# Expert tiles taken in pairs, second-layer products as 64-row halves, combine weights matched on VectorE

## The chip, the cores and the metric

One core of one Trainium2 chip runs one program. The metric is device time in microseconds from start to end of an execution, as the median over runs. The five engines named below are TensorE (PE, with its weight loads PEld), VectorE (DVE), ScalarE (ACT), GpSimd (POOL) and SyncE (SP), whose queue issues most transfers.

## The reference

A pre-norm decoder layer on x of shape (16, 128, 256), float32: `x + attention(norm(x))`, then cross attention over a context, then a mixture of experts. Only the last concerns the change:

```python
probs = softmax(x @ gate_w)                      # 2048 tokens, 64 experts
topk_w, topk_idx = top_k(probs, 8); topk_w /= sum(topk_w)
for each expert: hdn = silu(x @ gw) * (x @ uw)   # 256 -> 64
                 acc += combine[:, e] * (hdn @ dw)   # 64 -> 256
out = acc + sigmoid(x @ shared_gate) * shared_expert(x)
```

## The kernel before

The experts are computed sparsely. For each batch r of 128 tokens the router finds the top 8 experts, and GpSimd scatters the 128 normalised rows eight times, by indirect DMA, into the experts' blocks of the table xs (`cross_pool`, line 1824; 128 scatters, of which at most two are under way). A scatter's slot is the expert's start plus the token's rank in it, and the slots of batch r come from VectorE (`route_slots`).

The rows are then taken in 192 tiles of 128 rows: tiles 0 to 63 are the first blocks of the 64 experts (the pair order runs from the last experts to the first), tiles 64 to 191 the further blocks, wherever they lie; three small tables (line 2031, kept in line 2037) hold for each of these the first row and the places of its weights, which SyncE and TensorE load into registers (lines 2197 and 2227). SyncE loads a pair of tiles (`load`, lines 2154 and 2157) into one of four buffers. TensorE turns a tile (`turn`, L2237, two transpositions), ScalarE copies it to x_turned, TensorE makes gate and up side by side (`up`, L2247), ScalarE applies silu, VectorE multiplies (L2325), TensorE turns the hidden values (`turn_hidden`, L2256), VectorE copies them (L2331), TensorE multiplies them by the second-layer weights (`down`, L2264), ScalarE copies the rows to y_tile (L2306), and SyncE stores a pair (`store`, L2162) to the table ys, six pairs behind its loads. A float32 product is two passes on TensorE, a transposition one.

down_res holds the second-layer weights of an even expert on partitions 0 to 63 and of the odd one on 64 to 127. The hidden product is written twice, so that its transposition fills 128 rows; line 2331 multiplies it by 1 or 0 per half (`par`), and a product of 128 rows with both experts' weights gives the one wanted.

The order is written out by hand in loops over j, the tile, one for each engine: in iteration j TensorE turns tile j, makes up(j - 1), turn_hidden(j - 3), down(j - 5). VectorE's loop also holds the sorting of the output rows (`combine_rows` at j = 20), eight reductions of weights found by GpSimd, every sixth iteration, the shared expert's gates and the combines.

Output rows go back by 128 gathers (`combine_pool`, L2403): gather g = 8r + k takes the k-th expert's rows of batch r from ys, with at most three under way. Batch r needs the stores of the first 36 + 4r pairs; a ring of 32 tiles receives them. VectorE adds them to X with their weights (`combine`, L2459). Before the gathers GpSimd turns slots into rows of ys (lines 2371 to 2381, from tables that SyncE loads at pairs 4 and 8; the load for pair 8 stands behind its wait for `row_steps`) and, for each k, finds the weights by comparing with the sorted rows (lines 2388 to 2390). SyncE loads down_res (`between_loads`, L2474) after the last cross-attention product.

## Time and profile before

| what | value |
|---|---|
| median of 3 runs (lowest to highest) | 999.36 us (995.24 to 1002.95) |
| profiled execution, first to last instruction | 1000.0 us (no other time of it is given) |
| mean granted clock of TensorE | 0.895 of 2.4 GHz |
| busy: PE, PEld | 810.3, 640.0 us |
| busy: DVE, ACT, POOL | 654.2, 533.3, 581.4 us |
| chain that ended last | DMA 26%, PE 19%, POOL 7% |
| largest piece of the chain | scatters to xs, 19% |

Busy time is summed over the whole span, whose stages have different limits: a scatter stage until 694 us, a tile stage, and gathers. A matmul's duration in the rows is longer than its share of the stream, since matmuls overlap; what counts is the distance from one start to the next. In a timeline a row merges neighbours of one kind: start, length from first start to last end, engine, line, operation, output and inputs, count, and in brackets the idle time before it and what ended it.

### The profile page before, as it was taken

To read this page: it belongs to the slowest core of one execution; us is meant where nothing else is said; L and a number is where in the kernel's file an instruction comes from. 1 tells how busy PE (TensorE), PEld (TensorE's weight loads), DVE (VectorE), ACT (ScalarE), POOL (GpSimd) and SP (SyncE) were. 2 spreads that over 40 slices of the span, in tenths; PEclk is the share of its full clock that TensorE was granted. 3 is DMA by queue.
4 is the path that set the end of the run, shared out by engine and by line. 5 is a ranking of instruction groups with operands and counts; after the bars stand their busy time and mean duration, and the time that the engine had idled before them with its cause. 6 is when DMAs were issued, how large, how long until landed. Compare 5 with 4: busy or idle time off the path is not lost.

```text
span 1000.0 us, 21154 instructions
## 1 busy us (share of the span) xinstructions
PE 810.3 (81%) x6280; PEld 640.0 (64%) x6311; DVE 654.2 (65%) x1963; ACT 533.3 (53%) x1373; POOL 581.4 (58%) x768
## 2 busy tenths in 40 slices
PE   5988999999999999877787865224899999989702
PEld 3766777777777777655555533113789988888601
DVE  6747778787887786987777743241456567666545
ACT  2424677667766776655554443112567777666400
POOL 3685657666767862005653445465699355555665
PEclk9987999999999999989888887555999999999955
DMA  6200212222222113645547654524767799989635
GB/s 153 61 21 17 70 49 83 66 69 83 71 66 71 45 43 78 144 102 159 165 151 229 212 169 148 192 85 155 236 207 217 220 295 297 280 273 283 200 99 158
DMA packets 128908, 143.03 MB, mean 143 GB/s; under 512 B 25619, under 2 KB 114262, under 8 KB 128798
## 3 DMA queue, kind: packets, MB, share of 16 engines
q1 hardware_dynamic: 116510, 108.11, 36.6%
q0 software_dynamic: 12288, 33.57, 10.7%
q8 instruction: 55, 0.90, 0.4%
q14 instruction: 55, 0.45, 0.2%
HBM read 78.54 MB, written 62.93 MB: 141 GB/s over the span
## 4 chain that ended last, share of the span: by engine, by line
DMA 26%; PE 19%; POOL 7%; issue 7%; DVE 4%; ACT 1%; SPq 0%; POOLq 0%; another core or an unknown queue 0%; DVEq 0%; ACTq 0%
DMA xs<-xrow,slot_idx 19%; PE bank L2247 6%; PE bank L2264 5%; DMA got_rows<-ys,slot_idx 5%; POOL got_rows L2403 4%; PE bank L2237 3%; DVE xmax L1514 2%; POOL xs L1824 1%; PE bank L2256 1%; PE bank L1504 1%; PE bank L1581 1%; DMA ctx_in<-xs 1%; PE bank L1606 1%; DMA got_rows<-row_tables 0%; DVE X L2459 0%
## 5 line engine op out<-in xcount | busy, mean ns | idle before, releaser
L1824 POOL DMA_INDIRECT xs<-xrow,slot_idx x128 | 123.5, 965 | 111.9 <-DMA xs<-xrow,slot_idx 101.5
L2403 POOL DMA_INDIRECT got_rows<-ys,slot_idx x128 | 123.3, 963 | 92.0 <-DMA got_rows<-ys,slot_idx 45.3
L947 ACT ACTIVATE probs<-bank 128x512 f32<-128x512 f32 x192 | 113.9, 604 | 85.2 <-PE bank L759 48.1
L2247 PE MATMUL bank<-up_res,x_turned 128*128 (+1 forms) x768 | 121.0, 281 | 5.5 <-DVE hid_s L2325 5.0
L2325 DVE TENSOR_TENSOR hid_s<-gate_s,bank 128x128 f32<-128x128 f32 x192 | 54.8, 286 | 106.8 <-ACT gate_s L2299 105.5
L2264 PE MATMUL bank<-down_res,hid_t 128*128 (+1 forms) x384 | 114.8, 381 | 0.1
L1681 ACT ACTIVATE probs<-bank 128x512 f32<-128x512 f32 x128 | 75.6, 612 | 68.0 <-PE bank L1581 67.6
L2247 PEld LDWEIGHTS bank<-up_res,x_turned 128*128 128x128 f32 x768 | 103.1, 195 | 7.8 <-issue 5.9
L1514 DVE TENSOR_REDUCE xmax<-bank 128x2 f32<-128x512 f32 x128 | 85.2, 687 | 34.4 <-PE bank L1504 34.4
L2293 ACT COPY x_turned<-bank 128x256 f32<-128x256 f32 x192 | 72.5, 377 | 37.7 <-PE bank L2237 37.5
L2459 DVE SCALAR_TENSOR_TENSOR X<-got_rows,left,X 128x256 f32<-128x256 f32 x128 | 61.7, 482 | 40.9 <-DMA got_rows<-ys,slot_idx 38.2
L757 PE MATMUL bank<-query,keys 128*128 128x256 f32 x256 | 82.7, 347 | 0.5 <-ACT probs L947 0.4
L1504 PE MATMUL bank<-keys_x,query_x 112*128 112x256 f32 x256 | 58.6, 316 | 29.9 <-DVE xmax L1514 29.9
L1070 DVE TENSOR_REDUCE blockmax<-bank 128x32 f32<-128x512 f32 x96 | 63.1, 686 | 26.7 <-PE bank L709 25.5
L1504 PEld LDWEIGHTS bank<-keys_x,query_x 112*128 112x128 f32 x256 | 50.8, 212 | 41.3 <-DVE xmax L1514 32.5
L1581 PE MATMUL bank<-query_x,keys_x 114*128 114x512 f32 x128 | 68.5, 535 | 4.4 <-ACT probs L1681 4.1
L2306 ACT COPY y_tile<-bank 128x256 f32<-128x256 f32 x128 | 47.7, 373 | 40.9 <-PE bank L2264 40.4
L2331 DVE TENSOR_SCALAR hid_t<-bank,par 128x128 f32<-128x128 f32 x192 | 66.1, 344 | 0.1
L2264 PEld LDWEIGHTS bank<-down_res,hid_t 128*128 128x128 f32 x384 | 58.0, 191 | 0.9 <-issue 0.7
L1221 POOL TENSOR_TENSOR key_a<-keyT,kv_rows 64x512 bf16<-64x512 f32 x16 | 16.6, 1037 | 69.5 <-ACT keyT L900 69.5
L757 PEld LDWEIGHTS bank<-query,keys 128*128 128x128 f32 x256 | 49.2, 192 | 7.9 <-ACT probs L947 0.9
L2256 PE MATMUL bank<-ident,hid_s 128*128 128x128 f32 x192 | 52.7, 274 | 0.0
(366 smaller groups left out, 2158.1 us busy)
## 6 DMA issues: line engine op xcount, KB each, us to landing
ys<-y_tile SPq DMA_DIRECT2D x64, 256.0 KB
xs<-zero_b SPq DMA_DIRECT2D x16, 512.0 KB, 3.2
ys<-xn SPq DMA_DIRECT2D x32, 256.0 KB
up_res<-in_w_up SPq DMA_DIRECT2D x6, 1280.0 KB, 7.4
keys_x<-key_rows_x SPq DMA_DIRECT2D x32, 192.0 KB
ctx_in<-in_ctx SPq DMA_DIRECT2D x32, 128.0 KB, 2.4
key_rows_x<-ctx_hi SPq DMA_DIRECT2D x256, 16.0 KB, 1.5
query_x<-xq_rows_hi SPq DMA_DIRECT2D x64, 64.0 KB
```

The lines of the kernel that those rows point to most:

```text
L757: nc.tensor.matmul(o, keys[p][:, kvh * 4 + j, :], query[p][:, kvh, 256:512], start=True, stop=False)
L947: nc.scalar.activation(probs[:, u, :], SCORE[u % 2][:], ACT.Exp, scale=SCALE)\
L1504: last = nc.tensor.matmul(max_bank(g)[:, n * D:n * D + D], query_x[s][0:XROWS, k, pair // 2, c * 128:c * 128 + 128], keys_x[s][0:XROWS, k, ...
L1514: nc.vector.tensor_reduce(xmax[b % 2][:, m // 4, hs:hs + 2], max_bank(XH * b + m)[:].rearrange("p (h n) -> p h n", h=2), AX, ALU.max).then ...
L1581: nc.tensor.matmul(XSCORE[n % 2][:].rearrange("p (t m) -> p t m", t=2), keys_x[s][0:XROWS + 2, k, c * 128:c * 128 + 128], query_x[s][0:XRO ...
L1681: nc.scalar.activation(probs4[b % 2][:, u, :], XSCORE[n % 2][:], ACT.Exp, scale=XSCALE)\
L1824: nc.gpsimd.indirect_dma_start(out=xs, out_offset=bass.IndirectOffsetOnAxis(ap=slot_idx[:, r, k:k + 1], axis=0), in_=xrow[r % XROW_RING][: ...
L2247: last = nc.tensor.matmul(bank[2 + j % 2][:, 0:128], x_turned[j % 2][:, c * 128:c * 128 + 128], w[:, 256 * c:256 * c + 192].rearrange("p ( ...
L2264: nc.tensor.matmul(bank[6 + j % 2][:, 0:D], hid_t[j % 3][:], down_weights(j), start=True, stop=True).then_inc(S("tile_down"), 1)
L2293: nc.scalar.copy(x_turned[j % 2][:], bank[j % 2][:, 0:D]).then_inc(S("tile_kept"), 1)
L2331: nc.vector.tensor_scalar(hid_t[j % 3][:], bank[4 + j % 2][:, 0:128], par[:, 0, j:j + 1], None, ALU.mult).then_inc(S("tile_hidT"), 1)
L2403: nc.gpsimd.indirect_dma_start(out=got_rows[:, g % GOT_RING, :], out_offset=None, in_=ys[0:T * (E + 8 * r + 8), :], in_offset=bass.Indirec ...
```

## The change

The tile loops run over 96 pairs instead of 192 tiles: one keep (512 columns), one silu, one hidden product and one hidden copy for a pair, two buffers of each. The hidden product is written once per tile. In a pair of first blocks one transposition turns both tiles' hidden values, the even one's to partitions 0 to 63, the odd one's to 64 to 127, and `down` issues two products of 64 rows, one on each half, into different banks. In the other pairs each tile's hidden values are turned separately to partitions 0 to 63, and both second-layer products use that half; for these the odd experts' weights are loaded a second time to the lower half. The even tile's rows are copied by ScalarE, the odd one's by VectorE. The `par` table and what makes it are gone.

The weights of the combine are found on VectorE in the order of the slots (`match_weights`): 32 chunks of four batches and one k, 24 before the tile loop and one in each of iterations 2 to 9. So that the later sort of the output rows keeps that order, a multiple of 32768 per expert is added to the row's number and masked off again (`row_places`). The ring of gathers has 16 places instead of 32, a gather of k = 0 or 4 waits for the combine 12 before, and each combine waits for its own gather.

```diff
-ROWS_AT, WEIGH_GAP, COMBINE_AT = 20, 6, 97
-HIDDEN_AT, ADD_AT = 76, 104
+NP = TILES // 2
+GOT_RING = 16
+CHUNK = 4
+EARLY_CHUNKS, CHUNKS = 24, 32
+CHUNKS_AT, ROWS_AT, HIDDEN_AT, COMBINE_AT, ADD_AT = 2, 15, 24, 46, 90
+ROW_KEY = 32768
+Y_BEHIND = 7
...
             def down_weights(j):
-                return down_res[:, ds(256 * first_pair(j // 2) if j < E else down_at[j - E], 256)]
+                if j < E:
+                    return down_by[I * (j % 2):I * (j % 2) + I, first_pair(j // 2), j % 2, :]
+                return down_res[0:I, ds(down_at[j - E], 256)]
...
+            def turn_hidden(p):
+                pe.wait_ge(S("tile_hidden"), ended("tile_hidden") + p + 1)
+                if p >= 2:
+                    pe.wait_ge(S("tile_hidT"), ended("tile_hidT") + p - 1)
+                if 2 * p < E:
+                    nc.tensor.transpose(HID_TURNED[p % 2][:, 0:T], hid_s[p % 2][:].rearrange("p a i -> p (a i)"),
+                                        ident[:]).then_inc(S("tile_hid_turned"), 1)
+                    return
+                for a in range(2):
+                    last = nc.tensor.transpose(HID_TURNED[p % 2][0:I, T * a:T * a + T], hid_s[p % 2][:, a, :],
+                                               ident[:])
+                last.then_inc(S("tile_hid_turned"), 1)
+
+            def down(p):
...
+                pe.wait_ge(S("tile_hidT"), ended("tile_hidT") + p + 1)
+                if p:
+                    pe.wait_ge(S("tile_y"), ended("tile_y") + p)
+                if p >= 2:
+                    pe.wait_ge(S("tile_y_odd"), ended("tile_y_odd") + p - 1)
+                for a in range(2):
+                    turned = hid_t[p % 2][I * a:I * a + I, 0, :] if 2 * p < E else hid_t[p % 2][0:I, a, :]
+                    nc.tensor.matmul((Y_EVEN, Y_ODD[p % 2])[a][:, 0:D], turned, down_weights(2 * p + a),
+                                     start=True, stop=True).then_inc(S("tile_down"), 1)
...
+            for i in range(NP + 3):
+                if i < NP:
+                    values(i)
+                    turn(i)
+                if 0 <= i - 1 < NP:
+                    up(i - 1)
+                if 0 <= i - 2 < NP:
+                    turn_hidden(i - 2)
+                if 0 <= i - 3:
+                    down(i - 3)
...
+            for n in range(EARLY_CHUNKS):
+                match_weights(dve, n)
             g = 0
+            for i in range(1, NP + 4):
+                if i - 1 < NP:
+                    hidden(i - 1)
+                if 0 <= i - 2 < NP:
+                    hidden_turned(i - 2)
+                if 0 <= i - 4:
+                    rows_odd(i - 4)
+                if 0 <= i - CHUNKS_AT < CHUNKS - EARLY_CHUNKS:
+                    match_weights(dve, EARLY_CHUNKS + i - CHUNKS_AT)
...
+                while g < 8 * NS and COMBINE_AT + 18 * g // 25 <= i:
                     combine(dve, g)
                     g += 1
...
-            for k in range(8):
-                out = (a, c)[k % 2]
...
-                link(nc.gpsimd.tensor_tensor(out, v, t, ALU.subtract))
-                link(nc.gpsimd.tensor_scalar(out, out, 0.0, None, ALU.is_equal))
-                nc.gpsimd.tensor_tensor(out, out, routed[:, 0:NS, 0:E], ALU.mult).then_inc(S("weight_found"), 1)
...
-                if k == 0 and g >= GOT_RING:
-                    pool.wait_ge(S("combined"), ended("combined") + g - GOT_RING + 8)
+                if k % 4 == 0 and g >= GOT_RING:
+                    pool.wait_ge(S("combined"), ended("combined") + g - GOT_RING + 4)
...
+        def match_weights(dve, n):
+            lo, k = CHUNK * (n // 8), n % 8
+            some = slice(lo, lo + CHUNK)
...
+            at = slot_top[:, some, k:k + 1].to_broadcast([128, CHUNK, E])
+            route_link(dve, nc.vector.tensor_tensor(found, slot_of[:, some, :], at, ALU.is_equal))
+            route_link(dve, nc.vector.tensor_tensor(found, found, routed[:, some, 0:E], ALU.mult))
+            nc.vector.tensor_reduce(weigh[:, some, k], found, AX, ALU.add).then_inc(S("weight_taken"), 1)
...
+            def load_down(k, a, side, name):
+                some = slice(4 * k, 4 * k + 4)
+                sp.dma_start(down_by[I * side:I * side + I, some, a, :], halves[:, some, a, :]).then_inc(S(name), 16)
+
             for k in range(8):
...
+                if k == 6:
+                    sp.wait_ge(S("xpv_done"), B)
+                for a in range(2):
+                    load_down(k, a, a, "ld_down_res")
+            for k in range(8):
+                load_down(k, 1, 0, "ld_down_swap")
```

## Rows read from the trace of the kernel before

**Rows 1.** Stretches: length, busy us (instructions) of PE, PEld, DVE, ACT, POOL; clock; DMA; GB/s

```profile
820.00:860.00 40.00, 39.89 (x296) 35.98 (x294) 28.20 (x92) 28.30 (x99) 21.86 (x23) 1.00 0.94 291
960.00:1000.00 40.00, 7.68 (x16) 4.65 (x16) 21.00 (x40) 0.00 (x0) 23.53 (x25) 0.50 0.46 137
```

**Rows 2.** Chain of waits: start us, us, what; then TensorE's timeline at pair 8

```profile
691.50 2.88 DMA xs<-xrow,slot_idx
694.86 4.52 DMA got_rows<-row_tables
704.83 2.37 POOL got_rows L2376
707.60 5.48 DMA ctx_in<-xs
...
713.12 0.44 PE L2237 MATMUL bank<-ident,ctx_in 128*128 128x128 f32 x2 [1.55 <-DMA ctx_in<-xs]
```

**Rows 3.** TensorE's timeline, one tile: start us, us, engine, line, operation, count

```profile
760.60 0.38 PE L2237 MATMUL bank<-ident,x_tile 128*128 128x128 f32 x2
760.82 0.61 PE L2247 MATMUL bank<-up_res,x_turned 128*128 128x128 f32 x4
761.26 0.27 PE L2256 MATMUL bank<-ident,hid_s 128*128 128x128 f32 x1
761.37 0.60 PE L2264 MATMUL bank<-down_res,hid_t 128*128 128x256 f32 x2
761.80 0.38 PE L2237 MATMUL bank<-ident,x_tile 128*128 128x128 f32 x2
```

**Rows 4.** Timelines of SyncE's queue and GpSimd: the store and the first gather

```profile
789.01 0.38 SPq L2162 DMA_DIRECT2D ys<-xn  x1
...
792.01 1.06 POOL L2403 DMA_INDIRECT got_rows<-ys,slot_idx  x1 [13.91 <-DMA ys<-xn]
```

**Rows 5.** Gathers, line 2403: stretches with POOL busy (count); the line's durations

```profile
790.00:938.20 148.20, 83.95 (x88) 1.00 0.90 277
938.20:993.40 55.20, 39.32 (x41) 0.57 0.48 143
...
L2403 POOL DMA_INDIRECT got_rows<-ys,slot_idx x128: 940/946/1205, 792.0 to 992.4; - x128
```

**Rows 6.** Line 509: durations min/median/max ns, first and last start us, form

```profile
L509 PE MATMUL bank<-kv_masked,w x128: 374/374/478, 53.3 to 60.2; 32*128 32x256 f32 x128
```

**Rows 7.** TensorE's timeline in the shared expert

```profile
941.57 0.63 PE L2105 MATMUL bank<-ident,routed 128*64 128x128 f32 x4
942.13 1.99 PE L2120 MATMUL bank<-down_sh,up_res 64*128 64x256 f32 x8
944.05 0.63 PE L2105 MATMUL bank<-ident,routed 128*64 128x128 f32 x4
```

**Rows 8.** TensorE's waits from 713 to 938: total us, times, longest

```profile
PE bank L2247 <- DVE hid_s L2325: 5.0, 5, 1.8
```

**Rows 9.** Scatters, line 1824, by stretch: POOL busy (count), clock, DMA, GB/s

```profile
620.40:635.50 15.10, 4.79 (x5) 0.66 0.99 329
635.50:648.00 12.50, 8.64 (x9) 0.50 0.24 85
```

**Rows 10.** VectorE: first hidden product in its timeline; line 2077's durations

```profile
690.66 0.29 DVE L2325 TENSOR_TENSOR hid_s<-gate_s,bank 128x128 f32<-128x128 f32 x1 [23.66 <-ACT gate_s L2299]
...
L2077 DVE TENSOR_TENSOR routed<-routed,sig x4: 424/425/426, 794.1 to 808.8; 128x256 f32<-128x256 f32 x4
```

**Rows 11.** VectorE's timeline; chain of waits with GpSimd's issues beside it

```profile
952.06 4.15 DVE L2459 SCALAR_TENSOR_TENSOR X<-got_rows,left,X 128x256 f32<-128x256 f32 x8 [5.68 <-DMA got_rows<-ys,slot_idx]
...
951.60 0.95 POOL got_rows L2403
952.85 1.03 POOL got_rows L2403
954.19 0.96 POOL got_rows L2403
```

More of the change, by code:

```diff
@@ L1385, in build @@
         tiles_3 = sb("tiles_3", [3, EXTRA], I32)
[L1386 to L1390 removed]
+        tables_at.close()
+        place[0] = place.pop()
+        got_rows = sb("got_rows", [128, GOT_RING, D])
+        x_last = sb("x_tile3", [128, 2, D])
+        x_turned1 = sb("x_turned1", [128, 2 * D])
+        gate_s = [sb(f"gate_s{n}", [128, 2, I]) for n in range(2)]
+        hid_s = [sb(f"hid_s{n}", [128, 2, I]) for n in range(2)]
+        hid_t = [sb(f"hid_t{n}", [128, 2, T]) for n in range(2)]
         place[0].close()
@@ L2181, in sparse_loads @@
             batch_sent(sp, NS - 2)
-            for p in range(TILES // 2):
+            for p in range(NP):
                 if p < 4:
@@ L2202, in sparse_loads @@
                 load(p)
-                if p >= 6:
-                    store(p - 6)
-            for p in range(TILES // 2 - 6, TILES // 2):
+                if p >= Y_BEHIND:
+                    store(p - Y_BEHIND)
+            for p in range(NP - Y_BEHIND, NP):
                 store(p)
@@ new lines, in up @@
+            def up(p):
+                pe.wait_ge(S("tile_kept"), ended("tile_kept") + p + 1)
+                if p >= 2:
+                    pe.wait_ge(S("tile_hidden"), ended("tile_hidden") + p - 1)
+                for a in range(2):
+                    w = up_weights(2 * p + a)
+                    for c in range(2):
+                        both = w[:, 256 * c:256 * c + 192].rearrange("p (t i) -> p t i", i=I)[:, 0:3:2, :]
+                        last = nc.tensor.matmul(bank[2 + p % 2][:, 2 * I * a:2 * I * a + 2 * I],
+                                                x_turned[p % 2][:, a * D + c * 128:a * D + c * 128 + 128], both,
+                                                start=c == 0, stop=c == 1)
+                last.then_inc(S("tile_up"), 1)
@@ L2301, in rows_out, with keep @@
-            def rows_out(j):
-                act.wait_ge(S("tile_down"), ended("tile_down") + j + 1)
-                n = len(y_tile)
-                if j % 2 == 0 and j // 2 >= n:
-                    act.wait_ge(S(f"y_out{j // 2 % n}"), 16 * (j // 2 // n))
-                nc.scalar.copy(y_slot(j), bank[6 + j % 2][:, 0:D]).then_inc(S("tile_y"), 1)
-            for j in range(TILES + 6):
-                if 0 <= j - 6 < TILES:
-                    rows_out(j - 6)
-                if j < TILES:
-                    keep(j)
-                if 0 <= j - 1 < TILES:
-                    gate(j - 1)
+            def keep(p):
+                act.wait_ge(S("tile_turned"), ended("tile_turned") + p + 1)
+                if p >= 2:
+                    act.wait_ge(S("tile_up"), ended("tile_up") + p - 1)
+                nc.scalar.copy(x_turned[p % 2], X_TURNED[:]).then_inc(S("tile_kept"), 1)
@@ L2315, in sparse_scalar @@
+            for i in range(NP + 4):
+                if 0 <= i - 4:
+                    rows_even(i - 4)
+                if i < NP:
+                    keep(i)
+                if 0 <= i - 1 < NP:
+                    gate(i - 1)
             for n in range(4):
@@ L2449, in combine @@
                 dve.wait_ge(S("weights_ready"), ended("weights_ready") + 1)
-            if k == 0 and r < NS - 1:
-                for last in range(8 - GOT_AHEAD, 8):
-                    got_until(dve, g + last)
-            if r == NS - 1:
-                got_until(dve, g)
+            got_until(dve, g)
             if g:
```

311 lines of the change are left out of this document (138 added, 173 removed).

## The prediction

> **What bounds the kernel now.** I read the stretches of the span first [rows 1] (the loop holds the full clock and fills the DMA engines; behind it TensorE is nearly idle), then the chain of waits that ended last [rows 2], then single engines. Up to about 694 us the chain is GpSimd's 128 row scatters, each waiting for an earlier one; then three table loads and GpSimd's row arithmetic, which holds back the load of pair 8 (issued at 707.60, landed at 713) [rows 2]. From 713.1 to 938.2 TensorE runs the expert tiles almost without a gap at the full clock: from tile to tile 1.20 to 1.21 us, made of two transpositions (0.22), four first-layer passes (0.44), one hidden transposition (0.11) and two second-layer passes (0.43) [rows 3]. A pair of tiles is thus 2.42 us. The gathers of output rows start at 792.01, 3.0 us after the store of pair 35 was issued (at 789.01) [rows 4]; 88 of them are issued until 938.2 while the DMA engines are 90% busy, and 40 remain, at 1.36 us each (the last issue at 992.4) [rows 5]. So two things set the end: when the first 36 pairs are stored, and when the last pair is done. Everything else has slack.
>
> The span of 1000.0 us is 0.6 us above the median of the three runs; I make the sum against the span and take 0.6 off.
>
> **1. Second layer of the first 32 pairs, side by side.** Removed: one hidden transposition per pair, 0.11 us. Two products of 128 rows (4 passes of 0.2155, 0.86 us) become two of 64 rows on different halves of the array. Does the array run them together? The nearest row is the compression layer: 128 passes of 32-row products in four row groups, 256 columns each, start between 53.3 and 60.2 us [rows 6], one every 0.054 us, a quarter of 0.2155. I take two passes in the time of one: -0.43 us per pair. Bounds: nothing (-0) and -0.43.
> The pages give another answer. The Trainium skill ("TensorE: Matmul & The Clock Gate", Part 3, "The mechanism") says that matmuls are strict first-in first-out and only weight loads are pulled ahead. By it the first pass of the odd tile starts only with the second pass of the even one, three slots instead of two, and a pair saves 0.22 instead of 0.43. The row above speaks against it, since every product there is two passes too.
>
> **2. What the 64-row form costs in a stream of 128-row work.** The trace of before has this neighbourhood once, in the shared expert: four transpositions, then eight 64-row passes, then transpositions again [rows 7]. From 941.57 to 944.05 are 2.48 us, where 4 x 0.109 + 8 x 0.2155 make 2.16. Going into 64-row form and out again costs 0.32 us that the streams of [rows 3] don't have. (The Trainium skill, "TensorEngine Tiling (Array Packing)", "Key Properties", says that changing the tiling mode drains the engine; the rows give the price.) The new order does this once in every iteration, because the second layer of one pair stands between the hidden transposition of another and the turning of a third. Bounds: 0 to 0.35 (the weights behind it are 128 columns wide here, 64 there). I take 0.32.
> It is paid in all 96 pairs: the 64 extra tiles' pairs too use 64-row second-layer products, but both on the lower half, so nothing runs side by side. For them one hidden transposition of 128 columns becomes two of 64 (0.109 each in [rows 7]), two per pair as before.
> So a pair of first blocks takes 2.42 - 0.11 - 0.43 + 0.32 = 2.20 us, an extra pair 2.42 + 0.32 = 2.74 us.
>
> **3. The loop.** Pair 8 can't start earlier than today: its load stands on SyncE's queue behind the wait for GpSimd's row steps, and these hang on the scatters and the table loads, not on TensorE [rows 2]. What is gained in pairs 0 to 7 is therefore lost in that wait. From iteration 8: 27 iterations gain 0.22 (-5.9 us), and 64 (35 to 98) lose 0.32 (+20.5). TensorE waited 5.0 us for VectorE in five places [rows 8], mostly where VectorE stood in a combine that wants three gathers of a batch at once; the new combine follows 9 or more gathers behind its own, so I take 4.5 of it away. Sum **+10.1 us** on the last pair. The store of pair 35 (iterations 8 to 38) comes 5.9 - 1.3 = 4.6 earlier.
>
> **4. Second weight copy.** The second-layer weights now come in 24 loads of 256 KB instead of 8 of 512 KB: 2.1 MB more. While the 4.2 MB of before moved (620.4 to 635.5), GpSimd issued 5 scatters; in the 12.5 us after them 9 [rows 9]. Each loaded scatter takes 3.0 us, an unloaded one 1.4; half again as much data is 7.5 us more under load, 2.5 scatters slower by 1.6. But part of the loads now starts before the last cross-attention product, where other loads already slowed the scatters: I take **+2.8 us** (0 to 5). The scatters are the chain there, so all that follows moves.
>
> **5. Weights matched on VectorE.** Removed from GpSimd: 24 operations over the whole weight table, after which it waited 13.9 us for rows [rows 4], so it gains nothing at the end. Added to VectorE: 32 chunks of two products of 128x256 and one reduction. A product of this size is 0.425 us [rows 10]; for the reduction over as many elements I take the same, with the waits between them 1.36 us a chunk. 24 chunks, 33 us, stand ahead of the first tile, where VectorE idles from 667.0 to 690.7 [rows 10]. It comes 6 us late after the shift of part 4; then each of iterations 2 to 9 has 2.5 us of work on VectorE against 2.2 on TensorE. TensorE has room: pair 8 waits for its load anyway. Both come out within a microsecond of each other, so 0, with 3 us if the cover is short (queued behind the chunks are the hidden products, and TensorE's transpositions behind these).
> The chunks also meet the scatters. GpSimd's issue pitch goes from 1.25 to 1.34 us when VectorE combines two operands beside it [rows 11]; over the some 20 scatters of that time (28 us at 1.4) about **+1.0 us** (0 to 2). The Trainium skill ("GPSIMD Engine Reference", Specifications) names this contention for instructions of two SBUF inputs; it gives no price.
> The row key, the sorting in four parts, the smaller tables: a few operations of 0.2 us each beside TensorE's stream, 0. The copy of every odd tile's rows moves from ScalarE to VectorE; both are busy 28 of 40 us in the loop at its fullest [rows 1], and pairs halve the number of the other operations, so 0. One x_turned bank: its copy ends well before the next turning, 0. SyncE's store lies one pair further back but behind the same iteration, 0.
>
> **6. The tail.** The ring of 16 ties gather g to combine g - 12, and combines run at 18/25 iteration each, the last in the loop g = 74. So 88 gathers are out when the loop ends, as today, and 40 remain. The new waits are for single gathers, not batches: 1.30 instead of 1.36 us each, -2.4 us; and the last 9 combines, which today run back to back after 992.0, follow each landing, -1.4. **-3.8 us.**
>
> **Sum:** 1000.0 + 10.1 + 2.8 + 1.0 - 3.8 = 1010.1, less 0.6: 1009.5, written **1010 us**, about 1% slower.
>
> **Rivals.**
> (a) *The mode change is hidden* behind waits or weight loads in this stream. Then first pairs take 1.88, extra ones 2.42: -14.6 - 4.5 + 3.8 - 3.8 = -19.1 for the first sum; some 4 gathers more remain at the end (+5.2), since the loop is shorter than the gathers need: 1000 - 19.1 + 5.2 - 0.6 = 985.5, the other side. For it: each waiting product is issued long before it runs. Against it: [rows 7], at full clock and with their inputs ready. It decides below 0.10 us per iteration, where the loop's cost falls under its gain.
> (b) *Half the price*: 0.16 us per iteration, 995 us, no change.
> (c) *Strict order of passes*: 27 x 0.22 = 5.8 us more, 1015.
> (d) *VectorE becomes the bound* in iterations 2 to 10 or where chunks, sorts and combines meet: up to 6 us more, 1016; its busy time per pair leaves it little room early and a microsecond later.
> (e) *The change doesn't do what it says*: if the 64-row products don't run together at all, 27 x 0.43 more, 1021.
>
> **Chances.** My sum 0.47, (a) 0.18, (b) 0.17, (c) 0.08, (d) 0.06, (e) 0.04. The range 985 to 1020 takes in (a)'s centre, the bounds of parts 4 and 5 and (c), (d); my own case's range is 1002 to 1018. One per cent, about what a measurement of this kernel can tell from none, is 989.4 to 1009.4. My case lies on the upper edge: 0.30 of its 0.47 above, 0.17 within, where (b) lies too. Faster 0.18, within 1% 0.34, slower 0.48.
>
> **What would show it.** The start-to-start time of pairs: 2.20 for first blocks and 2.74 for extra ones (1.88 and 2.42 would be (a), 2.42 for the first (c)). Pair 8 near 717. The first gather near 791. The scatters' end at 698. VectorE's last early chunk near 700. The last tile near 952 with 88 gathers out. If the extra pairs take 2.42 us, I am wrong by the mode change; if pair 8 comes before 713, by the chain ahead of it.

## The result, and the profile after

The changed kernel takes **1028.33 us** (median of 4 runs, 1026.5 to 1033.1), the kernel before in the same job 1000.7 us: a ratio of **1.029, interval 1.025 to 1.034**. The prediction said 1010 and a range up to 1020: the direction was right, the size and the range were not. The two profiled spans are 1024.7 and 1000.0 us, so 24.7 us are to be placed. Four instants cut the span:

| | before | after | difference added by the stretch |
|---|---|---|---|
| last scatter issued | 691.5 | 703.1 | +11.6 |
| pair 8 turned | 713.1 | 725.5 | +0.8 |
| pair 9 turned | 715.6 | 730.1 | +2.0 |
| last expert product ends | 938.6 | 961.2 | +8.2 |
| end of the span | 1000.0 | 1024.7 | +2.1 |

**The scatters.** Two views of line 1834 (line 1824 before): the same two stretches, in the changed kernel and then before. Columns: POOL busy (number issued), clock, DMA share, GB/s.

```profile
609.00:643.00 34.00, 9.25 (x10) 0.59 1.08 236
643.00:690.00 47.00, 30.01 (x32) 0.50 0.26 90
```

```profile
609.00:643.00 34.00, 16.74 (x18) 0.64 0.64 209
643.00:690.00 47.00, 29.54 (x32) 0.50 0.27 93
```

Ten scatters in place of 18; behind them the rate is the same. Read share and rate together: the busiest part of before moved 329 GB/s at a share of 0.99 [rows 9], the changed kernel 236 GB/s at 1.08. The engines are fuller and move less. (With the loads of the changed kernel the last scatter came at 703.1, 700.6 and 699.2 us in three traces, in the kernel before at 691.5 and 690.1; so one trace places this term to within some 4 us.)

**The start of the loop.** VectorE's timeline of the changed kernel, and GpSimd's beside it:

```profile
677.94 0.40 DVE L2468 TENSOR_TENSOR got_rows<-slot_of,slot_top 128x256 f32<-128x256 f32 x1
...
711.00 0.47 DVE L2345 TENSOR_TENSOR hid_s<-gate_s,bank 128x128 f32<-128x128 f32 x2
...
717.61 1.25 DVE L2468 TENSOR_TENSOR got_rows<-slot_of,slot_top 128x256 f32<-128x256 f32 x1
718.89 2.46 DVE L2469 TENSOR_TENSOR got_rows<-got_rows,routed 128x256 f32<-128x256 f32 x1
721.39 0.42 DVE L2470 TENSOR_REDUCE count<-got_rows 128x4 f32<-128x256 f32 x1
721.73 0.28 DVE L2345 TENSOR_TENSOR hid_s<-gate_s,bank 128x128 f32<-128x128 f32 x1
```

```profile
716.23 2.35 POOL L2413 TENSOR_TENSOR got_rows<-got_rows 128x1024 f32<-128x1024 f32 x1
718.66 2.42 POOL L2415 TENSOR_TENSOR got_rows<-got_rows,slot_of 128x1024 f32<-128x1024 f32 x1
```

The 24 early chunks run until 711.0, though pair 0 was turned at 699.55 (690.66 was the first hidden product before [rows 10]). Then the chunks inside the loop meet GpSimd's row steps: the product of line 2469 takes 2.46 us in place of 0.42 and ends at 721.35, 0.27 us behind the end of GpSimd's operation (718.66 to 721.08). The product of line 2468 before it ends at 718.86, 0.28 us behind GpSimd's of 716.23 to 718.58. A hidden product is queued behind each. GpSimd's own operation is no longer than its neighbours.

Pair 8 hardly feels it. Its load is issued 15.9 us behind the last scatter (718.99; 16.1 in the kernel before), and it is turned 22.4 us behind the last scatter where it was 21.6. The next two chunk products, of 1.40 and 2.23 us, then hold up pair 9. The x buffers are used in the order ctx_in, ctx_hi, ctx_lo, x_tile, so ctx_in holds pair 8 and ctx_hi pair 9. TensorE in the changed kernel, and pair 9 in the kernel before:

```profile
725.54 0.66 PE L2240 MATMUL bank<-ident,ctx_in 128*128 128x128 f32 x4
...
728.80 0.33 PE L2262 MATMUL bank<-ident,hid_s 128*128 128x128 f32 x1 [1.71 <-DVE hid_s L2345]
729.42 0.70 PE L2282 MATMUL bank<-down_res,hid_t 64*128 64x256 f32 x4 [0.29 <-DVE xrow L2365]
730.06 0.66 PE L2240 MATMUL bank<-ident,ctx_hi 128*128 128x128 f32 x4
```

```profile
715.63 0.38 PE L2237 MATMUL bank<-ident,ctx_hi 128*128 128x128 f32 x2
```

The chain of waits runs there over VectorE (start, length, what) and releases pair 9, from which on every pair follows at its own pitch:

```profile
724.51 1.33 DVE got_rows L2468
725.87 2.25 DVE got_rows L2469
...
729.42 0.70 PE bank L2282 x4
```

**Pairs.** TensorE's timeline of the changed kernel, a first pair and an extra pair, to be read against [rows 3]:

```profile
762.56 0.27 PE L2262 MATMUL bank<-ident,hid_s 128*128 128x128 f32 x1
762.76 0.70 PE L2282 MATMUL bank<-down_res,hid_t 64*128 64x256 f32 x4
763.39 0.66 PE L2240 MATMUL bank<-ident,ctx_in 128*128 128x128 f32 x4
```

```profile
852.71 0.38 PE L2266 MATMUL bank<-ident,hid_s 128*64 128x128 f32 x2
853.02 1.13 PE L2282 MATMUL bank<-down_res,hid_t 64*128 x4
854.08 0.66 PE L2240 MATMUL bank<-ident,x_tile 128*128 128x128 f32 x4
854.57 1.06 PE L2252 MATMUL bank<-up_res,xrow 128*128 x8
```

Four passes side by side last 0.63 us from first start to the next operation, in series 1.06 us. So the halves of the array do work together. A 64-row pass itself is no slower than one of 128 rows: the eight passes of [rows 7] last 1.92 us and the four here 1.06, so four more cost 0.86, or 0.215 each. What the form costs lies at the change into it and out of it. Steady pairs follow each other every 2.222 us (first blocks) and 2.755 us (extra).

**The gathers**, line 2430 by stretch, up to the last product and behind it, and what GpSimd waited for at them (us, times); before are [rows 5]:

```profile
804.00:961.20 157.20, 84.01 (x85) 1.00 0.84 254
961.20:1019.00 57.80, 40.41 (x44) 0.58 0.47 142
```

```profile
L2430 POOL DMA_INDIRECT got_rows<-ys,slot_idx x128: 940/946/1201, 804.9 to 1018.9; - x128
...
  DVE X L2488: 31.3, 14
```

One gather (940/946/1201 ns) costs what it did, but from first to last issue they take 214.0 us, where they took 200.4. (A gather under way at 961.2 is counted in both stretches.) 31.3 us are waits for combines to give a buffer free; before these were 2.2 us. So a second way to add up the loss: first gather +12.9, the stream of gathers +13.6, behind it -1.8.

The first gather also stands further behind the loop than it did: 8.7 us behind the turn of pair 38, where it was 4.8 ([rows 4]; pair 38 turned at 787.21). It waits for the store of pair 35, and that store for VectorE's copy of the odd tile's rows, which the new loop makes one iteration behind ScalarE's copy of the even tile's (798.64). TensorE, VectorE and SyncE's queue in the changed kernel:

```profile
796.21 0.66 PE L2240 MATMUL bank<-ident,ctx_lo 128*128 128x128 f32 x4
...
801.40 0.40 DVE L2365 COPY xnT<-bank 128x256 f32<-128x256 f32 x1
...
801.88 0.38 SPq L2158 DMA_DIRECT2D ys<-xnT  x1
```

No run moved this copy, so what it costs in time is not shown.

### The profile page after: what moved, and what is told of

Read it like the earlier page. It is cut to its first block, busy times and chain, and to the rows that moved or that the text cites. A ratio compares the mean times of both kernels' runs of the same rounds, so it can differ in the third digit from the quotient of the medians.

```text
span 1024.7 us, 20489 instructions
## 1 busy us (share of the span) xinstructions
PE 820.2 (80%) x6246; PEld 619.4 (60%) x6277; DVE 675.3 (66%) x1947; ACT 483.4 (47%) x1085; POOL 529.1 (52%) x743
## 3 DMA queue, kind: packets, MB, share of 16 engines
q1 hardware_dynamic: 118814, 110.20, 37.1%
## 4 chain that ended last, share of the span: by engine, by line
PE 28%; DMA 17%; DVE 9%; issue 5%; POOL 4%; ACT 1%; POOLq 0%; another core or an unknown queue 0%; DVEq 0%; ACTq 0%
DMA xs<-xrow,slot_idx 16%; PE bank L2282 8%; PE bank L2252 8%; PE bank L2240 5%; POOL got_rows L2430 3%; DVE xmax L1524 2%; DVE got_rows L2469 2%; PE bank L2266 1%; DMA got_rows<-ys,slot_idx 1%; DVE got_rows L2468 1%; DVE count L2470 1%; POOL xs L1834 1%; PE bank L1514 1%; PE bank L1591 1%; PE bank L1616 1%
## 5 line engine op out<-in xcount | busy, mean ns | idle before, releaser
L2345 DVE TENSOR_TENSOR hid_s<-gate_s,bank 128x128 f32<-128x128 f32 x96 | 27.5, 287 | 105.6 <-ACT gate_s L2318 105.5
L2282 PE MATMUL bank<-down_res,hid_t 64*128 (+1 forms) x384 | 94.7, 411 | 0.8 <-DVE xn L2365 0.3
L2488 DVE SCALAR_TENSOR_TENSOR X<-got_rows,count,X 128x256 f32<-128x256 f32 x128 | 61.3, 479 | 30.6 <-DMA got_rows<-ys,slot_idx 26.1
L2282 PEld LDWEIGHTS bank<-down_res,hid_t 64*128 64x128 f32 x384 | 52.5, 185 | 22.7 <-issue 18.1
L2311 ACT COPY xrow<-bank 128x512 f32<-128x512 f32 x48 | 28.1, 585 | 56.4 <-PE bank L2240 56.4
L2252 PE MATMUL bank<-up_res,xrow 128*128 (+1 forms) x384 | 52.4, 281 | 0.0
L2252 PE MATMUL bank<-up_res,x_turned 128*128 (+1 forms) x384 | 51.2, 277 | 0.0
L2252 PEld LDWEIGHTS bank<-up_res,xrow 128*128 128x128 f32 x384 | 48.4, 198 | 0.0
L1875 PE MATMUL bank<-ident,xrow 128*128 128x128 f32 x32 | 9.9, 409 | 47.0 <-ACT xrow L1860 44.8
L2252 PEld LDWEIGHTS bank<-up_res,x_turned 128*128 128x128 f32 x384 | 47.1, 193 | 0.3 <-issue 0.3
```

Source lines behind the costliest of these rows:

```text
L2252: last = nc.tensor.matmul(bank[2 + p % 2][:, 2 * I * a:2 * I * a + 2 * I], x_turned[p % 2][:, a * D + c * 128:a * D + c * 128 + 128], both ...
L2282: nc.tensor.matmul((Y_EVEN, Y_ODD[p % 2])[a][:, 0:D], turned, down_weights(2 * p + a), start=True, stop=True).then_inc(S("tile_down"), 1)
L2488: nc.vector.scalar_tensor_tensor(X[:, r, :], got_rows[:, g % GOT_RING, :], weigh[:, r, k:k + 1], X[:, r, :], ALU.mult, ALU.add).then_inc(S ...
```

## The experiments

Theory: each loss above has its own cause (loads, chunks, 64-row products, the written-down pace of the combines). Rivals stand in the expectations. The code cuts are shortened. One slip runs through the expectations: the instants that they call pair 8's turn in a changed kernel (730.1, 724.0, 715.5) are those of pair 9, and only the 713.1 of the kernel before is pair 8's. Like goes with like at 715.6. The differences between changed kernels are not touched by it.

**Loads.** Run one: second copy later.

```
- for k in range(8): load_down(k, 1, 0, "ld_down_swap")      # between_loads
+ if p >= 10 and (p - 10) % 2 == 0 and (p - 10) // 2 < 8: load_swap((p - 10) // 2)   # sparse_loads, behind load(p)
```

> The eight loads of the second copy of the odd halves (2.1 MB to partitions 0 to 63) are moved from the stage of the scatters into the loop of pairs, one behind the x loads of pairs 10, 12, ... 24; the sixteen first-copy loads keep their form, 64 partitions each. The last scatter is issued at 691.5 us in the kernel before and 703.1 in the changed one. Theory A, the amount of data alone (6.3 MB in place of 4.2) held the scatters up: last scatter at 691 to 693, pair 8's turn at 718 to 720, the time some 11 us under the changed kernel's, about 1017. Theory B, the form of the loads (each to 64 partitions, so half as many partitions take twice the bytes) counts too: 4.2 MB at the 225 GB/s of the changed kernel last some 19 us, the scatters end at 695 to 699 and the time is about 1021 to 1024. Rival C, the scatters were held up by VectorE's early chunks and not by loads: no change, 703 and 1028. In the loop the eight moved loads should cost nothing, since the steady pair of 2.22 us is PE's own.

Measured: 1018.63 us, ratio 1.020 [1.017, 1.023]; last scatter 693.6, pair 9 at 720.7.

Run two: first copy to all partitions.

```
- for a in range(2): load_down(k, a, a, "ld_down_res")
+ sp.dma_start(down_by[:, some, 0, :], io["w_down"][some].rearrange("q p d -> p q d"))
  down_weights: down_by[I * (j % 2):..., first_pair(j // 2), 0, :]
```

> The sixteen first-copy loads of 256 KB to 64 partitions each become eight of 512 KB to all 128 partitions (the odd expert's rows of a pair now stand beside the even one's, in the same columns; the first pairs' second products read them there). The second copy stays where it is, eight loads to partitions 0 to 63. So the bytes are the same 6.3 MB, and 4.2 MB of them go in the form of the kernel before. Theory A (amount alone): last scatter still at 703, time about 1028. Theory B (form as well): the first 4.2 MB move at the 280 GB/s and more of the kernel before, the last 2.1 MB at about 225, the scatters end at 695 to 698, time about 1021. Rival C: no change.

Measured: 1023.02 us, 1.023 [1.021, 1.025]; last scatter 697.4, pair 9 at 724.6.

Run three: both edits.

> Both edits together: eight loads of 512 KB to 128 partitions in the stage of the scatters, as in the kernel before, and the second copy in the loop. Theories A and B both: the scatters end at 691.5 as before, the whole 11.6 us come back, the turn of pair 8 is at 718.5 (730.1 less 11.6) and the time about 1016 to 1017. Rival C (VectorE's early chunks held the scatters up): the last scatter stays near 703, the time near 1028. What is left over the kernel before, some 16 us, would then be the start of the loop (5), the extra pairs (6) and the tail.

Measured: 1014.08 us, 1.015 [1.012, 1.017]; last scatter 690.0, pair 9 at 715.5 (715.6 in the kernel before). The three kernels' scatters, in this order, in the stretch where the changed kernel issued 10:

```profile
609.00:643.00 34.00, 13.85 (x15) 0.61 0.79 197
```

```profile
609.00:643.00 34.00, 11.50 (x12) 0.64 0.87 248
```

```profile
609.00:643.00 34.00, 16.36 (x17) 0.60 0.58 201
```

Rival C falls: VectorE's early chunks stood in all of them. The whole delay is the loads' and comes back with them. From the corners of the four medians, the amount is worth 8.9 to 9.7 us of time and the form 4.6 to 5.3; run one lies nearer to the amount theory, the other theory's 695 to 699 was too late. The form also shows inside one trace. In run two the first copy goes to 128 partitions and then the second to 64, and here is a stretch of each (all five engines, then clock, DMA share, GB/s):

```profile
614.00:620.00 6.00, 1.71 (x14) 0.89 (x18) 0.00 (x0) 0.97 (x2) 1.92 (x2) 0.50 1.09 365
630.00:636.00 6.00, 0.00 (x0) 0.00 (x0) 0.00 (x0) 0.00 (x0) 0.96 (x1) 0.50 1.13 215
```

Smaller packets are not the reason: over the whole span the queue of the loads moves the same 110.20 MB in 118814 packets in run one and 118686 in run three. Why the same bytes take the engines longer when 64 partitions are written stays open.

**Chunks.**

```
- EARLY_CHUNKS, CHUNKS = 24, 32;  CHUNKS_AT, ROWS_AT, HIDDEN_AT = 2, 15, 24   # one chunk a step
+ EARLY_CHUNKS, CHUNKS = 18, 32;  CHUNKS_AT, CHUNK_STEP, ROWS_AT, HIDDEN_AT = 12, 2, 15, 25
```

> The loads stay as in the changed kernel. 18 early chunks stand ahead of the loop in place of 24, and the other 14 are matched at every second step from 12 on, behind GpSimd's six row steps; sorting, row places and the shared gates move to the odd steps behind them. Theory: the first hidden product no longer waits for 24 chunks until 711.0 (18 of 1.37 us end near 702.6), and no chunk meets a row step, which stretched the two-input operations from about 0.5 to 2.2 to 2.5 us. Pair 8 then turns 4 to 6 us earlier, at 724 to 726, and the time is 1022 to 1024. Rival, the chunks are covered and the start of the loop is set by the x loads behind the scatters: pair 8 stays at 730 and the time at 1028. Second rival, the 14 chunks in the loop make VectorE the bound of their pairs (1.37 plus about 1.1 us in a pair of 2.22): each costs up to 0.25 us, 3.5 us in all, and the time is 1026.

Measured: 1024.75 us, 1.025 [1.023, 1.028]; last scatter 700.6, pair 9 at 724.0, the first hidden product at 703.24 right behind its gate. The chunk's second product in the changed kernel and here (ns min/median/max):

```profile
L2469 DVE TENSOR_TENSOR got_rows<-got_rows,routed x32: 424/425/2465, 678.4 to 733.6; 128x256 f32<-128x256 f32 x32
```

```profile
L2471 DVE TENSOR_TENSOR got_rows<-got_rows,routed x32: 424/425/491, 674.7 to 793.4; 128x256 f32<-128x256 f32 x32
```

Away from GpSimd's row steps no product is longer than 0.49 us. From last scatter to pair 9 are 23.4 us in place of 27.0 (24.1 before). The 14 chunks in the loop cost no pair anything.

Loads and chunks together:

> The loads of both edits (first copy to 128 partitions, second copy in the loop) and the chunks moved (18 early, 14 at every second step from 12 on). With the loads mended the last scatter was issued at 690.0 us and pair 8 turned at 715.5; with the chunks moved pair 8 turned 23.4 us behind the last scatter (724.0 and 700.6) where it was 25.5 with the loads alone. Theory: the two are independent, pair 8 turns at 713.4, as in the kernel before (713.1), and the time is 1010.5 to 1012. What is left over the kernel before, some 11 us, is then all from behind pair 8: 64 pairs of 2.755 us and the tail. Rival, the x loads of the first pairs share the queues with something that the chunks had covered: pair 8 at 715 and no gain, 1014.

Measured: 1010.09 us, 1.012 [1.009, 1.015]; last scatter 687.7, pair 9 at 711.2: the start is that of the kernel before, or better (4.4 us earlier, of which 3.8 are an earlier last scatter). About 18 of the 28 us are explained by these two; the remaining 10 are from behind pair 9 (10.6 in the trace).

**Extra pairs without the change of mode.** The upper halves hold zeros and any weights:

```
- turned = hid_t[p % 2][0:I, a, :]                     down_res[0:I, ds(down_at[j - E], 256)]
+ turned = hid_t[p % 2][:, a, :]                       down_res[:, ds(down_at[j - E], 256)]
+ if 2 * p < E + 4: route_link(dve, nc.vector.memset(hid_t[p % 2][I:128], 0.0))   # first two extra pairs
+ load_swap: both halves, 16 loads
```

> The kernel with loads and chunks mended, and the second layer of the 64 extra pairs as products over all 128 rows: the upper 64 rows of the turned hidden tiles hold zeros, the second copy is loaded to both halves (16 loads in the loop), and PE no longer changes between 128-row and 64-row products in the extra pairs; the first pairs keep their two products side by side. Theory: of the 2.755 us of an extra pair, 0.32 to 0.34 are the way into the 64-row products and out of them; a pair is then 2.42 (two tiles of 1.209 in the kernel before), 64 x 0.335 = 21.4 us less, the last product ends at 923 to 925 and the time is about 989. Rival 1, the price is not of the change of mode but of a weight load that nothing hides, which 128 rows have as well: 2.6 us and more, 1000 or above. Rival 2, VectorE with its combines becomes the bound of the shorter pair: between 990 and 1000, with waits for hidden tiles in the trace.

Measured: 998.87 us, 1.000 [0.998, 1.003]. An extra pair in steady stream:

```profile
867.49 0.38 PE L2275 MATMUL bank<-ident,hid_s 128*64 128x128 f32 x2
867.71 1.03 PE L2291 MATMUL bank<-down_res,hid_t 128*128 x4
868.58 0.60 PE L2249 MATMUL bank<-ident,ctx_lo 128*128 128x128 f32 x4
869.01 1.06 PE L2261 MATMUL bank<-up_res,x_turned 128*128 x8
869.91 0.38 PE L2275 MATMUL bank<-ident,hid_s 128*64 128x128 f32 x2
```

The distance is 2.42 us (2.414 over many pairs), 0.34 under the changed kernel's. Into the products 0.22 us in place of 0.31, the products 0.87 in place of 1.06, the transpositions behind them 0.43 in place of 0.49: 0.34 in all. This settles the price: 64 x 0.34 = 21.8 us of TensorE's time. Rival 1 is dead. But only 11 of the expected 21 us arrived. Two reasons show. Pairs 9 to 24 lasted 2.5 to 3.3 us at eight places, 5.4 us too long in all, where the second copy (now 4.2 MB) passes; and the end is not the loop's any more. From first to last issue the gathers take 201.9 us, 12.5 less than with loads and chunks mended (214.4), and no less than before.

**The pace of the combines**, on the padded kernel and on the changed one:

```
- while g < 8 * NS and COMBINE_AT + 18 * g // 25 <= i:      COMBINE_AT = 46, ADD_AT = 90
+ while g < 8 * NS and COMBINE_AT + 1 * g // 2 <= i:        COMBINE_AT = 47, ADD_AT = 108
```

> The kernel with padded extra pairs, and the combines (and with them the 16 buffers that the gathers fill) at a quicker pace: combine g stands at step 47 + g/2 in place of 46 + 18g/25, so 104 of 128 are in the loop in place of 73. In the changed kernel 85 gathers were out when the last product ended, and the other 43 took 1.32 us each behind the loop. Theory: gathers, which went at 1.84 us each in the loop because they waited for buffers that VectorE had not combined yet, go at 1.25 to 1.45; some 104 to 110 are out at the last product's end, the tail is 20 x 1.32 = 26 us shorter, and the time is 960 to 968. Rival 1, the gathers are themselves the limit in the loop (a pair of 2.42 us asks for two combines, 1.21 us each, and 1.25 is the best pitch seen): VectorE waits for them and stalls PE, the loop lasts up to 10 us longer, and the time is 970 to 978. Rival 2, descriptors' making on GpSimd is slowed by VectorE's two-input combines: the pitch stays at 1.6 and more, and the time near 985.

> The changed kernel as it is, with the quicker pace of combines alone (47 + g/2; the shared products' adds from combine 108 on in place of 90). A pair of 2.755 us asks for a gather every 1.38 us, above the best pitch seen of 1.25. Theory: the 43 gathers behind the loop become some 22, 21 x 1.32 = 28 us less, and the time is 1000 to 1004, level with the kernel before. So the tail of the changed kernel, which should have become shorter, stayed because of the pace in which the combines are written down. Rival, the pace in the loop is that of the gathers (GpSimd's descriptors beside VectorE's two-input operations, 1.6 to 1.8 us each): VectorE then waits in the loop, PE stalls, and the time is 1020 or more.

Measured: 1002.49 us (1.003 [1.000, 1.005]) and 1012.43 us (1.015 [1.011, 1.019]). In both, 104 gathers are out when the last product ends, as expected, but that end is late: 964.8 and 971.8. The gathers by stretch, changed kernel with the quicker pace:

```profile
802.00:971.80 169.80, 101.55 (x104) 0.99 0.84 251
971.80:1003.00 31.20, 22.05 (x24) 0.50 0.59 176
```

And what VectorE waited for in the padded kernel with the quicker pace (us in total, times, longest):

```profile
DVE X L2501 <- DMA got_rows<-ys,slot_idx: 54.5, 49, 3.5
```

Rival 1 of both holds: VectorE stands in combines whose rows have not landed, and TensorE behind it. The stream of gathers lasts 200.4 and 200.5 us. In seven undisturbed traces (two of the kernel before, five with other paces or shorter pairs) it lasts 199.1 to 201.9 us, and in the six that keep the written pace at 2.755 us a pair 214.0 to 214.9. No pace brought it lower, so it acts as a floor: first gather, some 200 us of gathers, some 6 to 8 behind. The quicker pace alone gives back 16 us of the changed kernel's loss: 13.5 by the stream, the rest by a first gather that came 2.4 us earlier behind an earlier last scatter (699.2), which the pace has no hand in.

**Spread loads, a middling pace, four gathers under way.** Edits on the padded kernel: one load of the second copy behind each of the pairs 9 to 24; combine g at 46 + 2g/3; GOT_AHEAD 4 in place of 3.

> The kernel with padded extra pairs (998.9 us), where the sixteen loads of the second copy stand one behind the x load of each of the pairs 9 to 24 in place of two behind every second from 10 on. In the run before, pairs 9 to 24 lasted 2.5 to 3.3 us at 9 of 16 places, 5.4 us above 16 x 2.22 in all, and PE's waits there had no late engine beside them. Theory: SyncE's two loads in a row kept the store behind them back, and the buffers of y came free late; spread, the pairs last 2.22 to 2.4, the last product ends 3 to 5 us earlier against the last scatter, and the time is 994 to 996. Rival: the bytes themselves (4.2 MB beside x loads and stores) delay the stores wherever they stand: no change, 999.

> As the spread kernel, and combine g at step 46 + 2g/3 in place of 46 + 18g/25: 1.61 us to a gather at pairs of 2.414, beside the 1.63 that gathers reached in the loop when the combines asked for one every 1.21 us. Theory: gathers keep up just so, 86 to 88 are out at the loop's end in place of 82, each is worth the 1.35 us of one behind the loop, and the time is 4 to 7 us under the spread kernel's. Rival: every late gather now stops VectorE and with it PE, the loop grows by as much as the tail shrinks, and the time is the same within 2 us.

> As the kernel before it in this list, and GpSimd may have four gathers under way in place of three (the gather g waits for gather g-4). In the loop 28 to 39 us of its waits were for the third gather back. Theory: the landing of a gather is what sets the pitch, so with four under way it falls from 1.63 to 1.4 in the loop and from 1.37 to 1.25 behind it; the tail is 3 to 6 us shorter and the time 4 to 8 us less. Rival: the queues' work sets the pitch and not the latency, so that gathers land as late as before and wait longer: no change within 2 us.

Measured 1039.82, 1039.71 and 1045.51 us, beside a kernel before of 1081.35 (1078.8 to 1089.7): ratios 0.958, 0.961, 0.967. The kernel before is slow here too, so the cause is in none of the edits, and nothing of this job can be set beside 998.9. Within it the middling pace changes nothing and four gathers under way are 6 us slower. Two of the kernels once more, with the padded and the changed one:

> The spread kernel once more, on whichever chip comes. On the chip of the run before, the kernel before took 1081 us in place of 1000, so nothing of that run can be set beside the padded kernel's 998.9. Theory of the spread loads: 994 to 996 beside a kernel before of 1000, and 3 to 5 us under the padded kernel in this job. Rival: the same as the padded kernel within 2 us.

> The padded kernel once more, beside the spread one on the same chip. Expected 999 and a ratio of 1.00 to the kernel before where that takes 1000. Where the kernel before takes 1081, as on the other chip, 1040 to 1044 and a ratio of 0.96.

> The kernel with spread loads and combines at 46 + 2g/3 once more. Theory: 3 to 7 us under the spread kernel of this job, so 989 to 993 beside a kernel before of 1000. Rival: the loop grows by what the tail loses, the same as the spread kernel within 2 us, as on the other chip (1039.7 and 1039.8).

> The changed kernel itself in the same job, so that all five stand side by side. Where the kernel before takes 1000, a ratio of 1.029 as recorded. Where it takes 1081: the other chip's extra time lies, by the traces there, in the loop once gathers, stores and x loads run together, where PE waited for stores; a pair of 2.755 us leaves more room for transfers than one of 2.42, so the ratio should be smaller than 1.029, between 0.98 and 1.02.

Measured: 1038.84, 1030.12, 1028.46 and 1047.87 us, the kernel before 1073.68 (1056.9 to 1082.7), on a chip on which it had taken 999.4 in an earlier job. The changed kernel's ratio is 0.982 [0.966, 0.998] here: under 1, but by less than 2%, so unclear as a verdict. The spread loads are 9 us slower than the padded kernel in this job. In the trace of the changed kernel the early stages are 5.8 us late (pair 9 at 735.8, and still 5.8 at pair 42); some 20 us more lie in the loop from pair 42 on, when gathers run. The stretch 830 to 900 in the changed kernel, undisturbed and here (columns as in [rows 1]):

```profile
830.00:900.00 70.00, 70.00 (x461) 55.15 (x460) 38.47 (x110) 31.66 (x77) 37.31 (x37) 1.00 0.88 265
```

```profile
830.00:900.00 70.00, 62.70 (x380) 48.58 (x378) 32.67 (x93) 24.63 (x63) 31.06 (x32) 0.93 0.73 219
```

Fewer bytes at a lower share, and TensorE is idle for 7.3 of 70 us. A byte costs the DMA engines the same share in both (301 and 300 GB/s at a full share), so they are less used, not less efficient; what they wait for is not shown. A last job:

> Spread loads, padded extra pairs and combines at 46 + 2g/3. Where the kernel before takes 1000 us: 989 to 995, a ratio of 0.990 to 0.995, if the theories of the spread loads and of the pace both hold; 999 (1.00) if neither. Where it takes 1075: 1028 to 1040 again, a ratio of 0.96 to 0.97.

> The kernel before, traced in the same job. Where it takes 1000 the trace is the one shown ahead. Where it takes 1075, the trace tells where the 75 us lie: in the loop behind the first gather, as in the changed kernel (there +20 us of +25), if transfers are what is slow; in all stages alike, if it is a clock.

> Spread loads and padded extra pairs, the combines' pace as it was. Where the kernel before takes 1000: 994 to 996 if two loads in a row held the stores back, 999 if the bytes do. Where it takes 1075: 1039 again.

It was undisturbed: 1002.12 (1.002 [0.999, 1.006]), 999.96 (0.999 [0.996, 1.003]) and 1006.11 us (1.005 [1.001, 1.008]). The theory of two loads in a row asked for 994 to 996 and falls. What is left is its rival, the bytes, which no run varied by themselves in this kernel. DMA shares from pair 9 on, with 2.1 MB, 4.2 MB, and 4.2 MB spread:

```profile
711.00:762.00 51.00, 51.00 (x395) 39.62 (x391) 34.86 (x124) 27.75 (x69) 1.88 (x1) 1.00 0.93 279
```

```profile
709.00:760.00 51.00, 46.24 (x352) 35.85 (x351) 30.03 (x110) 23.70 (x62) 1.74 (x1) 1.00 1.03 297
```

```profile
719.00:770.00 51.00, 45.96 (x345) 35.00 (x342) 29.60 (x109) 21.71 (x61) 0.42 (x1) 1.00 1.05 287
```

At 0.93 TensorE has no gap, at 1.03 it loses 4.8 of 51 us. The middling pace gave 4 us against the spread kernel, and stays 3 us above the padded one's: no win. Four gathers under way was only tried in a disturbed job (stream 236.4 us against 232.4) and stays open, as does what holds the gathers at 200 us. No version beat the kernel before in an undisturbed job; the padded one equals it. Why the kernel before loses more than the changed one where transfers are slow stays open too: it was not caught in a trace there.

## Why the prediction was wrong

The forecast was +10.1 us on the span, the trace shows +24.7. The miss lies in two terms, step 4 (the second copy) and step 6 (the tail).

**Steps 1 and 2: right, to 0.02 us.** 2.20 and 2.74 us were forecast, 2.222 and 2.755 measured. Side by side holds, (a), (b) and (e) fall by it, and so does (c): the strict order of "TensorE: Matmul & The Clock Gate" in the Trainium skill would have shown first pairs of 2.42 us; the four passes in 0.63 us speak against it for products on different halves. The 0.32 us read from one place in the shared expert [rows 7] was the price of every iteration, as "TensorEngine Tiling (Array Packing)" in the Trainium skill lets expect of a drain; the padded pairs measured it again, 0.34.

**Step 3, the loop: +10.1 forecast, +10.2 measured, in part by luck.** From pair 8's turn to the last product are 225.4 us before and 235.6 after. Between the turns of pairs 9 and 95 and behind them 26 steps at 2.222 us gain 4.9, 60 at 2.755 lose 20.3 (0.338 each), and the last products run 1.6 us longer. The kernel before lost 8.8 us there to steps longer than its pitch of 2.417 us; the new loop loses nothing. I took away 4.5, from the one row of 5.0 us [rows 8]; the view of named waits under-counts such time, length less pitch times count gives it all. Against these 4.3 us too much stand 2.0 between pairs 8 and 9 that I did not foresee, and 2.4 by which pitches and last products come to more than my 14.6. The errors cancel.

**Step 4, the second copy: the failed step.** +2.8 us (0 to 5) forecast, +11.6 measured (8 to 12 with the other traces of these loads); with both edits of the loads 14.3 us of time come back, and the last scatter is where it was. I priced more data of the old form, and let some of it start early beside other loads for nothing. But each load now writes 64 partitions, and share and rate show that it moves fewer bytes in a full DMA time (236 GB/s at 1.08 against 329 at 0.99; inside one kernel 215 at 1.13 against 365 at 1.09). The early part was no relief either: the slow stretch runs from 609 to 643 us in place of 620 to 635. The upper bound of 5 was extrapolated from data alone; the form had no row before, and should have widened the range. The amount was under-priced too: the runs give it about 9 us and the form about 5.

**Step 5, the chunks: right up to pair 8, with 2 us behind it.** Cover 0 and contention 1.0 were forecast, +0.8 measured up to pair 8: its load is issued as far behind the scatters as before, and TensorE's stream, late by the chunks, comes to it within about a microsecond of its old place, as I had argued. The early chunks' duration was right (33 us from 677.9 to 711.0), their start was late by nearly the whole delay of the scatters. The contention I looked for stood at the wrong neighbour: not GpSimd's scatters, whose rate from 643 to 690 us is unchanged (32 in 47 us in both), but its row steps of 2.4 us, which stretch VectorE's two-input products to 2.46 us and make pair 9 2.0 us later. The Trainium skill's "GPSIMD Engine Reference" (Specifications) names this contention; the trace shows that in this meeting it was VectorE that paid. This is rival (d) in small, at its "2 to 10" iterations; moving the chunks gives 3.6 us back.

**Step 6, the tail: the second failed step.** -3.8 us forecast, +2.1 measured. I counted 88 gathers out and found 85, so the last gather is issued 57.7 us behind the last product in place of 53.9 (+3.8, where I had -2.4); behind it are -1.8, near my -1.4. The ring of 16 and the pace of 18/25 steps were in the text, but not that a step is 2.74 us in an extra pair: 0.72 x 2.755 = 1.98 us per combine, slower than the 1.67 at which the gathers went before. The ring turned the loop's slower steps into 31.3 us of waits, and the quicker pace takes them away (stream 200.5 us, span 1008.7). Of my rivals only (a) spoke of what the gathers themselves need, and only for a shorter loop.

Sum of the terms, in the prediction's order: +10.2 (loop) +11.6 (copy) +0.8 (chunks) +2.1 (tail) = 24.7, against +10.1 +2.8 +1.0 -3.8 = +10.1. The first two steps, on which I had put the doubt, were right; the terms about what lies around the loop made the miss.

## What to carry to other kernels

Price a load by its form as well as its bytes: DMA share and GB/s, read side by side, tell whether full engines also move much. When the rate of a loop changes, recompute every schedule that is written in its steps (here combines and, by a ring, gathers). After each repair ask which stream has the next longest run of its own: 21.8 us taken from TensorE brought 11, in part because in no run did the gathers take less than 199 us from the first on. And when two profiles are compared, check that an instant is the same pair in both, here by the name of its buffer.

## What the runs showed of the hardware

- A switch into 64-row products and back costs 0.34 us in a steady stream, where both sides are 128-row work: 0.09 on the way in, 0.19 from the first pass to the transpositions behind, 0.06 in these. Within the form further passes cost 0.215 us each, as at 128 rows. The same products padded to 128 rows cost nothing extra (2.414 us a pair, 2.417 before).
- Two-pass products on the two row halves, issued one after the other, ran together: four passes in 0.63 us against 1.06.
- Beside GpSimd operations over 128x1024 elements (2.4 us), VectorE's products of two SBUF inputs took up to 2.46 us in place of 0.42, ending 0.27 to 0.29 us behind GpSimd's end; GpSimd's six row steps took 14.6 us in all beside them and 14.4 in the kernel before.
- Loads that write 64 partitions moved 215 GB/s at a DMA share of 1.13, loads that write all 128 moved 365 at 1.09, in one kernel (run two); runs that differ in this form alone (one and three) moved the same bytes in as many packets to 0.1%.
- For whole jobs the kernel before took 1074 to 1081 us in place of 1000, once on a chip that had given 999 in an earlier job, and the changed kernel's ratio to it was 0.982 there in place of 1.029. Only the kernel before in the same job makes such numbers readable.
